# Macaron feed-forward and attention block on one core: splits, bounced writes and attention units shifted between steps, and the last step's units put behind its low part

## The reference

```python
x = x + 0.5 * ffn(layernorm(x), W1, W2, W3)
x = x + attention(layernorm(x), wq, wk, wv, wo, inv_freq)
x = x + 0.5 * ffn(layernorm(x), W1, W2, W3)

def ffn(x):        # hidden size 2048
    return fwht(silu(x @ W1.T) * (x @ W3.T)) @ W2.T
def attention(x):  # per token: the 16 heads of one token attend to each other
    q, k = rope(x @ wq.T), rope(x @ wk.T); v = x @ wv.T
    scores = einsum('bshd,bstd->bsht', q, k) / sqrt(32)
    return einsum('bsht,bstd->bshd', softmax(scores), v) @ wo.T
```

## Time and profile before

| | |
|---|---|
| Median of 3 runs | 2495.41 us (2487.95 to 2495.76) |
| The profiled execution, its own time | 2491.28 us |
| Its span, first to last instruction | 2489.5 us |
| PE busy | 2476.1 us (99%), 10983 matmuls |
| DVE busy | 2064.6 us (83%) |
| ACT busy | 530.4 us (21%) |
| POOL busy | 62.7 us (3%) |
| Granted TensorE clock, mean | 1.000 |

### The profile page before, as it was taken

One profiled execution on the slowest core, in us unless ns is written; L12 is line 12 of the kernel. 1 busy time (PEld: TensorE's weight loads), 2 busy tenths in 40 slices (PEclk: granted clock), 3 DMA queues, 4 the chain that ended last, 5 costly groups with the idle time before them and its releaser, 6 DMA issues.

```text
span 2489.5 us, 29950 instructions
## 1 busy us (share of the span) xinstructions
PE 2476.1 (99%) x10983; PEld 2047.7 (82%) x10983; DVE 2064.6 (83%) x2630; ACT 530.4 (21%) x792; POOL 62.7 (3%) x109
## 2 busy tenths in 40 slices
PE   9999999999999999999999999999999999999999
PEld 7888888888888888878888888888888888888887
DVE  9569889798987998979879898798887989888711
ACT  3332212222111221122211122112221112211211
POOL 0030000000000000000000000000000000000000
PEclk9999999999999999999999999999999999999999
DMA  9655736457474674646735667465572555635364
GB/s 343 251 193 195 233 147 218 144 207 255 153 224 128 239 237 169 216 137 239 257 97 195 194 240 245 139 224 161 206 252 94 193 187 219 211 110 194 141 217 165
DMA packets 169429, 489.89 MB, mean 197 GB/s; under 512 B 29056, under 2 KB 84608, under 8 KB 134784
## 3 DMA queue, kind: packets, MB, share of 16 engines
q1 hardware_dynamic: 81792, 419.73, 47.1%
q10 hardware_dynamic: 87552, 69.09, 10.1%
HBM read 430.06 MB, written 58.72 MB: 196 GB/s over the span
## 4 chain that ended last, share of the span: by engine, by line
PE 87%; DVE 8%; DMA 2%; issue 1%; ACTq 1%; ACT 1%; POOL 0%; SPq 0%; DVEq 0%; POOLq 0%
PE gu L652 19%; PE gu L654 19%; PE gu L653 19%; PE acc L683 7%; PE acc L687 7%; PE acc L684 7%; PE acc L652 3%; PE acc L653 2%; PE acc L654 2%; DVE mixed L1412 1%; DVE prod L1403 1%; DMA sub_squares<-prod 1%; DMA tile_squares<-tok 1%; DVE gated L1695 1%; PE acc L783 1%
## 5 line engine op out<-in xcount | busy, mean ns | idle before, releaser
L652 PE MATMUL gu<-xt,w_up 128*128 128x512 f32 x2048 | 798.5, 390 | 0.2
L654 PE MATMUL gu<-xt,w_up 128*128 128x512 f32 x2048 | 796.8, 389 | 0.0
L653 PE MATMUL gu<-xt,w_up 128*128 128x512 f32 x2048 | 796.7, 389 | 0.0
L652 PEld LDWEIGHTS gu<-xt,w_up 128*128 128x128 f32 x2048 | 384.4, 188 | 80.5 <-issue 0.8
L654 PEld LDWEIGHTS gu<-xt,w_up 128*128 128x128 f32 x2048 | 384.4, 188 | 80.2
L653 PEld LDWEIGHTS gu<-xt,w_up 128*128 128x128 f32 x2048 | 384.4, 188 | 79.7
L683 PE MATMUL acc<-w_down,hid 128*128 128x512 f32 x896 | 348.5, 389 | 0.0
L684 PE MATMUL acc<-w_down,hid 128*128 128x512 f32 x896 | 348.5, 389 | 0.0
L1695 DVE TENSOR_TENSOR gated<-gated,gu 128x512 f32<-128x512 f32 x240 | 163.0, 679 | 209.6 <-PE gu L654 187.1
L1155 ACT ACTIVATE hid<-gated 128x512 fp32r<-128x512 f32 x240 | 151.9, 633 | 784.7 <-DVE gated L1695 784.7
L1398 DVE TENSOR_TENSOR prod<-tok 128x1024 f32<-128x1024 f32 x256 | 309.1, 1219 | 1.3
(11 more groups left out here) (151 smaller groups left out, 1933.8 us busy)
## 6 DMA issues: line engine op xcount, KB each, us to landing
w_up<-up_pairs SPq DMA_DIRECT2D x240, 1024.0 KB, 4.9
w_down<-down_pairs SPq DMA_DIRECT2D x240, 512.0 KB, 3.7
up_pairs<-w_up SPq DMA_DIRECT2D x16, 1024.0 KB, 5.0
xt<-tile_squares ACTq DMA_DIRECT2D x48, 256.0 KB, 9.1
tile_squares<-tok ACTq DMA_DIRECT2D x10, 1024.0 KB, 8.8
prod<-up_raw SPq DMA_DIRECT2D x16, 512.0 KB, 6.3
down_pairs<-w_attn SPq DMA_DIRECT2D x4, 2048.0 KB, 17.7
out<-x ACTq DMA_DIRECT2D x7, 1024.0 KB, 5.4
```

Of the source, the lines that this page charges most:

```text
L652: nc.tensor.matmul(o, w_hi, m_hi, start=first, stop=False)
L653: nc.tensor.matmul(o, w_hi, m_lo, start=False, stop=False)
L654: return nc.tensor.matmul(o, w_lo, m_hi, start=False, stop=last)
```

## The change

Seven things are edited.

1. `units_ahead`: up to three units stand before the first h of a pass, where the pass is not in `WO_AT`; before it was at most two everywhere. By the tables that this gives, passes 1, 2, 4, 6, 9, 11 and 13 go from 2 to 3, the others stay at 2. In pass 2 the third of them is unit 7 of sub 2, so its exp goes from step 1 to before the first Silu. The spread over the steps follows: pass 2 from 2,3,3,2,3,3,2,1,2,2,2,1,3,3,2,0 to 3,2,3,2,3,2,2,2,2,1,2,2,2,3,2,0.
2. The last steps: step 14's units behind the low part are kept back as `rest`. If it is at most one, it is made before h of step 15, which is where it stood. If it is two, both are made behind the low part of step 15, and so before `moved_sub_low` and L1671. Step 14 has three units, and `rest` is two, in passes 1, 3, 5, 6, 8, 9, 12 and 13.
3. `X_SPLIT` goes from 13 to 14: ACT's casts L998 stand behind the moves of step 14 and before Silu of step 15.
4. For passes 5 and 7 `keep_squares` is replaced by two writes of a pair of subs (`keep_pair`), with runs of 64 elements, in steps 9 and 10.
5. There, norm and transpose go through `prod` as for the other passes, and into `tok` by pairs.
6. `writes_to` counts two writes for them instead of four.
7. `keep_output` of step 15 (passes 4, 7 and 10) goes behind `moved_sub_high` instead of ahead of it.

```diff
-    return sum(SUBS if q in TWICE else 1 for q in MOVED if q <= p)
+    return sum(2 if q in TWICE else 1 for q in MOVED if q <= p)
-X_STATS, X_APPLY, X_KEEP, X_MOVE, X_SPLIT = 6, 8, 10, 11, 13
+X_STATS, X_APPLY, X_KEEP, X_MOVE, X_SPLIT = 6, 8, 10, 11, 14
@@ units_ahead
-    mine = UNITS.get(p, ())
-    if len(mine) < 2:
-        return 0
-    return 1 if mine[1][1] == PIECES and mine[0] == (mine[1][0], PIECES - 1) else 2
+    mine, count = UNITS.get(p, ()), 0
+    while count < min(2 if p in WO_AT else 3, len(mine)):
+        g, u = mine[count]
+        if u == PIECES and (g, PIECES - 1) in mine[:count]:
+            break
+        count += 1
+    return count
@@ ACT, keep_squares and keep_pair
-                if p in TWICE:
-                    for s in range(SUBS):
-                        act.dma_start(tile_squares.rearrange("p (f s j) -> p f s j", s=SUBS, j=32)[:, :, s, :],
-                                      normed(s).rearrange("p (f j) -> p f j", j=32)).then_inc(s_squares_kept, 16)
-                else:
-                    act.dma_start(tile_squares, turned).then_inc(s_squares_kept, 16)
+                act.dma_start(tile_squares, turned).then_inc(s_squares_kept, 16)
+            def keep_pair(p, half):
+                act.wait_ge(s_turned, SUBS * MOVED[p] + 2 * half + 2)
+                act.dma_start(tile_squares.rearrange("p (f h c) -> p f h c", h=2, c=64)[:, :, half, :],
+                              turned_pair(half).rearrange("p (f c) -> p f c", c=64)).then_inc(s_squares_kept, 16)
@@ ACT, feed_forward
-                    for g in OUTPUT_KEEP.get((p, n), ()):
+                    for g in OUTPUT_KEEP.get((p, n), ()) if n < HT - 1 else ():
                         keep_output(g)
-                    if after in MOVED and n == X_KEEP:
+                    if after in TWICE and n in (X_KEEP - 1, X_KEEP):
+                        keep_pair(after, n - X_KEEP + 1)
+                    elif after in MOVED and n == X_KEEP:
                         keep_squares(after)
...
                         for g in early_subs(after):
                             moved_sub_high(g)
+                    for g in OUTPUT_KEEP.get((p, n), ()) if n == HT - 1 else ():
+                        keep_output(g)
@@ DVE, beside, after in TWICE
-                                ln_apply(key, s, normed(s), normed(s))
+                                if s >= 2:
+                                    dve.wait_ge(s_turned, SUBS * MOVED[after] + s - 1)
+                                ln_apply(key, s, square_source(s), src[:, s, :])
                             for s in pair:
                                 dve.wait_ge(s_ln, ln_done(key, s))
-                                squares = normed(s).rearrange("p (f j) -> p f j", j=32)
-                                nc.vector.transpose(squares, squares).then_inc(s_turned, 1)
+                            for s in pair:
+                                nc.vector.transpose(turned_pair(s // 2).rearrange("p (f s j) -> p f s j", s=2, j=32)[:, :, s % 2, :],
+                                                    square_source(s).rearrange("p (f j) -> p f j", j=32)).then_inc(s_turned, 1)
@@ DVE, feed_forward
+                    if n == HT - 1 and rest < 2:
+                        unit(rest)
                     dve.wait_ge(s_silu, n0 + n + 1)
...
-                    unit(count - min(count, 1))
+                    if n == STEPS - 1:
+                        rest = count - min(count, 1)
+                    else:
+                        unit(rest if n == HT - 1 and rest > 1 else count - min(count, 1))
```

More of the change, by code:

```diff
@@ L479, in build, with turned_pair @@
         turned = tok[:, 12:16, :].rearrange("p a n -> p (a n)")
+        def turned_pair(half):
+            return tok[:, 12 + 2 * half:14 + 2 * half, :].rearrange("p a n -> p (a n)")
         def by_token(ap):
```

## The result

The kernel after takes 2500.69 us (median of 11 runs, 2498.28 to 2504.71), the kernel before beside it 2494.24 us (11 runs, 2487.95 to 2498.13). The ratio is 1.0025, with a 95% interval of 1.0013 to 1.0036: slower by 6.45 us, within the 0.3% that I had called no change. The profiled execution took 2499.61 us with a span of 2497.8, against 2491.28 and 2489.5 before: 8.3 us more.

The account below looks back on a forecast made before the run. PE, busy 99% of the span, was taken as the bound. Terms +6.2, +1.7, -0.2, -0.65 and -0.4 sum to +6.6 us, 2497.9 from the profile or 2502.0 from the median; forecast 2499.5 us, range 2493 to 2507.

Parts of the forecast that it names:

- pass 1: 1.04, and transposes 3.14 - 0.88: Behind pass 1, all 3.40 us of the moved units go into PE's existing wait for the transposes: +3.4 us.
- passes 5, 8, 12: Behind these passes the first query waits 1.06 us for L1291, queued behind the moved units: +3.2 us together.
- behind pass 13: The four L1269 shift by 1.76 us, and the projection that needs them starts late: +1.1 us.
- pass 6: 1.04 - 2.25: Moved units let down(15) start 2.25 us earlier; the query then waits 1.06; Silu maybe a little late: -1.0 us.
- pass 9: 1.04 - 2.30: With the units gone down(15) starts 2.25 us earlier, the query then waits 1.06 us: about -1.2 us.
- pass 2, first steps: The third unit's exp precedes the first Silu, so PE waits in down(1) for step 1's low part: +1.7 us.
- pass 4: Two writes for four clear the backlog by step 15 and its wait of 0.64 us: -0.65 us.
- pass 7: Without the output's write beside it, the read L1291 waits for lands earlier: -0.4 us (0 to -0.9).
- The clock: Rival: longer pauses behind pass 1 halve the clock for some 4 us of work: +2, in all +8.6 us; chance 0.08.
- Late Silu in pass 6: Rival: step 15's Silu late behind issues and casts: +1.4 instead of -1.0, in all +9.0 us; chance 0.22.
- Late landings: Rival: shorter queue and later output write remove waits for late reads at pass ends: up to -4 us; chance 0.14.
- term of 0 for the casts: Casts one step later fit before step 15's gate is ready, so they cost nothing, except in pass 6.

Follow-up runs that it names:

- The run with four writes: Kernel before with the last-step edit and the casts in step 14, its four writes for passes 5 and 7 kept: 2502.83 us, one execution.
- the first set: Experiments around the last-step edit; beside them 35 executions of the unchanged kernel before, 33 undisturbed, median of all 2495.37 us.
- gap version: Kernel after, last units before h, in passes 6 and 9 behind the additions; pass 2: two ahead, casts in step 13: 2486.06 us (0.9961), again 2487.04 us (0.9964).

## Why the prediction was right, and where not

Term by term, in the profiled executions (us, stalls of PE by starts):

| term | forecast | measured |
|---|---|---|
| pass 1: 1.04, and transposes 3.14 - 0.88 | +3.4 | +3.30 |
| passes 5, 8, 12 | +3.2 | +3.12 |
| pass 3: 1.04 - 0.21 | +0.7 | +0.83 |
| behind pass 13 | +1.1 | +1.07 |
| pass 6: 1.04 - 2.25 | -1.0 | -1.21 |
| pass 9: 1.04 - 2.30 | -1.2 | -1.26 |
| pass 2, first steps | +1.7 | +1.59 |
| pass 2, end | -0.2 | -0.18 |
| pass 4 | -0.65 | -0.65 |
| pass 7 | -0.4 | -0.03 |
| lower clock behind pass 1 | 0 | +1.55 |
| sum | +6.6 | +8.1 |

**The mechanism held.** The last-step edit is the loss, alone and by its absence. It holds because the moved work is 3.4 us and the idle time it left was for the most part not on PE's path, while the place it went to was. The gain of 2.25 us in pass 6, which the forecast gives to this edit, can be had twice: the edit alone takes that wait away, and with the units put back the other edits do.

**The number is in part luck.** Between the profiled executions the change is 8.3 us and not 6.6; the missing term is the clock, and the sum with that rival, +8.6, is the nearer one. The time forecast, 2499.5, had 1.6 us added for the spread of the runs, which happens to stand in for the clock's 1.55. The medians differ by 6.45 us because the median of before lies 3.0 us above its profile and that of after 1.1.

**Pass 2.** The size was right and the place not: the forecast compared only the low part of step 1 with what PE wants. The first low part, which it starts at 346.55, ends at 347.24, and PE wants it at 346.1 (in before, down(0) starts at 344.26, and 8 matmuls come ahead of the first use), so most of the stall stands in down(0), a place not named. The sum is the same, since a wait in down(0) is taken off the one in down(1). The drain that the Trainium skill (ScalarE: Activation LUTs, "What ACT_TABLE_LOAD costs") adds to the load would have made the stall 3.1. The rows above show Silu at 346.66, 0.01 us behind a load of 1.28 us from 345.37; the stall is 1.59. The trace disagrees with the page on this point, and the sum without the drain was right.

**Late Silu in pass 6** cost nothing in after; it was some 0.5 us late and within the slack. The run with four writes has the wait, the one with two has not, which fits the reason given, though two more edits differ between them.

**The clock** was a rival at 0.08 and came true, in the profiled execution and, by the mean clock listed (0.999), in 9 of 11 runs of after. It came with its price (forecast +2, measured +1.55). My evidence against it was two pauses of 2.1 us at full clock in one execution. That was too little: of 33 runs of before in the first set 20 list a clock under 1.000, so the clock did fall within this kernel, outside the profiled execution; behind which pause, those runs do not show. In after it was pass 1's: with only that pass put back, 2 of 12 runs list less than 1.000. The Trainium skill (TensorE: Matmul & The Clock Gate, Part 1) has the gate follow recent activity; after agrees, with 0.50 behind its pauses, and the run with two units ahead in pass 2 shows the same pauses at 1.00. That the 6.45 us between the medians is less than 8.3 probably has a like reason: the kernel before, too, loses to falls and late landings in runs that were not profiled.

**Pass 7** gained nothing. The read landed as late without the output's write beside it, so that write was not what held it. What does was not tried.

**Late landings** I had as a cause that the shorter queue would remove. Whether it did anything in after is open: its 11 runs lie within 6.4 us and the 11 of before beside them within 10.2, but its profile has no gain from it. In the gap version, all 12 and all 6 runs that count list 1.000 and lie within 5.3 and 1.8 us, against 19.5 and 15.4 us for the 33 and 31 of the kernel before (more runs, and so wider for that alone). My term of 0 for the casts was right for a profile without late landings and may have missed a gain in the median: with the two writes 1.8 us by the medians and 0.16% by the ratios, whose intervals overlap (table above). That version does not stop late landings, but leaves slack in front of them; this reading is argued from the pass 3 and pass 9 rows, not shown for every run.

## What to carry to other kernels

An idle gap of a second engine was free room for work here; "behind the last low part" was not, because the next thing the first engine waits for stands in the same queue. Before moving work out of a stall, list every later place in that queue and its slack, and look for one where the work fits: here it was behind the additions, not before h nor behind low. And judge a small change by what an unlucky DMA does to it, since a single profile may show none.

## What the runs showed of the hardware

- Behind PE's pauses the granted clock sometimes goes to 0.50. It did after stalls of 2.01, 2.09, 2.36, 2.76, 3.14 (three kernels), 3.61, 3.78 and 4.42 us; it did not after 2.25 and 2.30 us in before, nor in one execution after 3.14. The traces have the fall between 0.7 us before PE went on (after the 3.78) and 1.4 us behind it (after the 2.01). The low stretch lasted 3.41 us and cost 1.2 to 1.7 us; at the 3.78 us of stall it lasted 6.83 us and cost 2.9.
- Four writes of 128-byte runs, one right behind the other, hold ACT's queue for 8.57 us; two of 256-byte runs of the same data, a step apart, for 1.16 us. The first of the four takes 0.61 us, so short runs alone do not hold the queue. Which of the length of the runs, the number of writes and the step between them counts was not tried.
- A write of `sub_squares` issued by 1529.9 us landed at 1542.9; in the profiled execution of after PE did not wait for it at all. The same kernel's runs differ by up to 19.5 us.
